# Router work between attention tiles in another order on every engine, and the gates of the first ten tiles on GpSimd

## The reference

```python
x = x + gat(layernorm(x), adj)      # h = n @ W.T + b_W
    # e[i,j] = leaky(h[i]@a1 + h[j]@a2 + b_a), masked by adj, softmax over j, @ h
x = x + moe(layernorm(x))           # logits = n @ Wr + br, the top 2 of 64 experts
    # gates = softmax of the two logits; per expert relu(n @ W1 + b1) @ W2 + b2
    # out = sum over both experts of gate * expert(n)
```

## Time and profile before

| | |
|---|---|
| median of 3 runs | 276.75 us (276.5 to 277.84) |
| profiled execution | 275.88 us, of which the span is 274.1 us |
| granted TensorE clock, mean | 0.925 |
| TensorE busy | 225.7 us (82%) |
| VectorE busy | 207.5 us (76%) |
| ScalarE busy | 179.6 us (66%) |
| GpSimd busy | 166.7 us (61%) |

### The profile page before, as it was taken

One profiled execution on the slowest core, in us unless ns is written; L12 is line 12 of the kernel. 1 busy time (PEld: TensorE's weight loads), 2 busy tenths in 40 slices (PEclk: granted clock), 3 DMA queues, 4 the chain that ended last, 5 costly groups with the idle time before them and its releaser, 6 DMA issues.

```text
span 274.1 us, 6240 instructions
## 1 busy us (share of the span) xinstructions
PE 225.7 (82%) x1863; PEld 214.7 (78%) x1863; DVE 207.5 (76%) x587; ACT 179.6 (66%) x425; POOL 166.7 (61%) x212
## 2 busy tenths in 40 slices
PE   1494899999988999369893569999999999999840
PEld 1354899999978999259782449999999999999740
DVE  6879999999999999913844714889886767666465
ACT  2748989999878978083351516787877777777400
POOL 5870003450879998972878745445888888875600
PEclk9999799999999999957997557999999999999995
DMA  6987664689477570199011122222159710100067
GB/s 160 205 163 148 133 115 79 163 224 236 149 194 196 153 285 22 40 420 383 22 40 43 57 60 63 61 81 58 51 151 312 253 38 33 41 31 29 23 202 268
DMA packets 11120, 36.89 MB, mean 135 GB/s; under 512 B 2256, under 2 KB 2832, under 8 KB 10320
## 3 DMA queue, kind: packets, MB, share of 16 engines
q0 software_dynamic: 5232, 14.98, 23.6%
q1 hardware_dynamic: 5424, 21.11, 22.5%
q10 hardware_dynamic: 432, 0.40, 0.6%
HBM read 39.36 MB, written 5.51 MB: 164 GB/s over the span
## 4 chain that ended last, share of the span: by engine, by line
PE 57%; DVE 21%; issue 6%; DMA 5%; POOL 5%; ACT 2%; SPq 1%; ACTq 1%; POOLq 0%; DVEq 0%
PE bank L1127 16%; PE bank L1139 16%; PE bank L1023 11%; DVE arena L746 6%; PE bank L1007 5%; DVE arena L740 5%; DMA arena<-result 2%; DMA xs<-in_x 2%; POOL table L431 2%; PE bank L972 2%; DVE arena L731 2%; PE bank L1116 1%; PE bank L1042 1%; PE bank L961 1%; DVE rank L790 1%
## 5 line engine op out<-in xcount | busy, mean ns | idle before, releaser
L1023 PE MATMUL bank<-arena 128*128 128x130 f32 x512 | 64.3, 284 | 0.0
L1023 PEld LDWEIGHTS bank<-arena 128*128 128x128 f32 x512 | 62.0, 199 | 0.6 <-ACT arena L577 0.4
L1127 PE MATMUL bank<-arena 128*128 x384 | 60.4, 281 | 0.5 <-ACT arena L642 0.5
L1139 PE MATMUL bank<-w2s,arena 128*128 x384 | 58.8, 276 | 0.2 <-issue 0.2
L1127 PEld LDWEIGHTS bank<-arena 128*128 128x128 f32 x384 | 51.6, 196 | 1.0 <-issue 0.9
L431 POOL DMA_INDIRECT table<-rows_in,pos x32 | 42.4, 1324 | 14.4 <-issue 7.8
L1139 PEld LDWEIGHTS bank<-w2s,arena 128*128 128x128 f32 x384 | 50.6, 192 | 0.6 <-issue 0.6
L899 DVE SCALAR_TENSOR_TENSOR arena<-bank,arena 128x128 f32 x96 | 33.6, 350 | 21.7 <-PE bank L1139 20.2
L647 ACT ACTIVATE arena<-bank,arena 128x128 f32<-128x128 f32 x96 | 35.2, 366 | 18.4 <-PE bank L1127 17.2
L655 ACT ACTIVATE arena<-arena 128x256 f32 x96 | 39.0, 408 | 2.3 <-issue 2.2
L577 ACT ACTIVATE arena<-bank 128x512 f32<-128x512 f32 x64 | 33.8, 596 | 10.2 <-PE bank L1007 10.1
(11 more groups left out here) (195 smaller groups left out, 286.3 us busy)
## 6 DMA issues: line engine op xcount, KB each, us to landing
arena<-in_adj POOLq DMA_DIRECT2D x16, 512.0 KB, 6.6
w2s<-in_w SPq DMA_DIRECT2D x8, 768.0 KB, 4.4
arena<-in_w SPq DMA_DIRECT2D x6, 1024.0 KB, 8.1
arena<-in_w SPq DMA_DIRECT2D x4, 512.0 KB, 5.8
w2s<-in_w SPq DMA_DIRECT2D x4, 512.0 KB, 4.0
xs<-in_x SPq DMA_DIRECT2D x4, 256.0 KB, 6.3
arena<-result SPq DMA_DIRECT2D x2, 512.0 KB, 4.4
arena<-result SPq DMA_DIRECT2D x4, 256.0 KB, 6.0
```

The lines of the kernel that those rows point to most:

```text
L1023: ins = pe.matmul(OB[t % 2][:, 0:D + 2], pt_r[:, t % 2, j, :], h[:, j, :], start=(j == 0), stop=(j == T - 1))
L1127: ins = pe.matmul(hp(p, b), w1u[:, p % UW, P * b:P * b + P], xT_all[:, bass.ds(column, P)], start=True, stop=True)
L1139: ins = pe.matmul(yp(p), hT[:, p % UH, b, :], w2s[:, bass.ds(u, 1), b, :].rearrange("p e d -> p (e d)"), start=(b == 0), stop=(b == HB - 1))
```

## The change

Nothing is computed differently but the first factor of the gates. The edits:

- **VectorE:** top2(q) of groups 0 to 2 moves ahead of leaky in the step (step 8, 12, 14), place(q) behind leaky of the same step, not one step later. Leaky(15) goes ahead of residual(13), and behind it come residual(13), top2(3), residual(14), place(3), top2(4), place(4), residual(15), top2(5) and so on. The gates of groups 0 to 2 leave VectorE.
- **GpSimd:** a new `gates(q)` for groups 0 to 2: 1 + ge, a power of -1, the product and the copy into the rows, after `counts` in steps 8, 12, 14. In each step the scatters now stand first. They move: tile 3 from step 12 to 11, tiles 5 and 6 from 14 to 13, and tile 9 from behind rstd_of(6) to step 15, ahead of it. Rstd_of(7) no longer stands behind tile 9's scatters.
- **ScalarE:** route_b(q) of groups 0 to 2 before evac, not after it. Norm(10) and norm(11) behind evac(13), no longer ahead of it, and so ahead of scores(15). Deviation(13) behind evac(14). After the loop another order of the last groups.
- **TensorE:** route_c(q) of groups 0 to 2 ahead of turn(LAST+4), not behind the attend before it or a step later; route_a(3) behind attend(13), route_b(3) ahead of attend(14), route_a(4), route_b(4) and route_a(5) in attend(15), route_c(5) ahead of group 6. Group 5's logits get a bank of their own (bank 0), as group 6's have.

New tensors and semaphores are left out of the diff.

```diff
@@ -23,9 +23,9 @@
...
     LAST = [START[q + 1] - 1 for q in range(NG)]
-    PLACED = [(0, 0, 9), (0, 1, 10), (0, 2, 11), (0, 3, 12), (1, 4, 13), (1, 5, 14), (1, 6, 14), (1, 7, 15), (2, 8, 15)]
-    NORMED = [(5 + 2 * i, 2 * i) for i in range(5)] + [(14, 10)]
-    LATER = [LAST[q] + 1 if q < 3 else LAST[q] for q in range(NG)]
+    PLACED = [(0, 0, 9), (0, 1, 10), (0, 2, 11), (0, 3, 11), (1, 4, 13), (1, 5, 13), (1, 6, 13), (1, 7, 15), (2, 8, 15), (2, 9, 15)]
+    EARLY = 3
+    NORMED = [(5 + 2 * i, 2 * i) for i in range(5)]
     LNS = [(t, t + 2) for t in range(0, T - 2, 2)] + [(T - 2, T - 1), (T - 1, T)]
@@ -175,14 +175,15 @@
...
         pos = sb("pos", [P, T, TOPK], I32)
-        gd = sb("gd", [P, GRP])
-        ge = sb("ge", [P, GRP])
-        gs = sb("gs", [P, GRP])
+        gd = sb("gd", [P, T])
+        ge = sb("ge", [P, T])
+        gs = sb("gs", [P, T])
+        minus = sb("minus", [P, T])
         gate = sb("gate", [P, TOPK, T])
...
         OB, M0, M1 = bank[4:6], bank[6], bank[7]
-        LB, RB = [M0] * (NG - 1) + [bank[1]], [M1] * (NG - 1) + [bank[2]]
+        LB, RB = [M0] * (NG - 2) + [bank[0], bank[1]], [M1] * (NG - 1) + [bank[2]]
         ends, coded, sides, b1_at = bank[0][0:E, 0:3], bank[4][0:1, 0:2 * WORDS], bank[5], bank[3][:, 0:HB * TAB]
@@ -377,6 +380,7 @@
...
             pool.memset(expo[:, :], -0.5)
+            pool.memset(minus[:, :], -1.0)
             link(pool.memset(ident[:, :], 0.0))
@@ -424,6 +428,16 @@
...

+            def gates(q):
+                rows = slice(START[q], START[q + 1])
+                pool.wait_ge(s_ge, q + 1)
+                link(pool.tensor_scalar(gs[:, rows], ge[:, rows], 1.0, None, ALU.add))
+                pool.tensor_tensor(gate[:, 0, rows], gs[:, rows], minus[:, rows], ALU.pow).then_inc(s_inv, 1)
+                pool.wait_ge(s_inv, q + 1)
+                pool.tensor_tensor(gate[:, 1, rows], ge[:, rows], gate[:, 0, rows], ALU.mult).then_inc(s_weights, 1)
+                pool.wait_ge(s_weights, q + 1)
+                link(pool.tensor_copy(rows_out[:, rows, :, GATE_COL], gate[:, :, rows].rearrange("p k g -> p g k")))
+
             def place(q, t):
@@ -446,18 +460,20 @@
...
             for s in range(T):
+                for q, t, at in PLACED:
+                    if s == at:
+                        place(q, t)
                 if s + 5 < T:
...
                 for q in range(COUNTED):
-                    if s == LATER[q] + 4:
+                    if s == LAST[q] + 5:
                         counts(q)
-                for q, t, at in PLACED:
-                    if s == at:
-                        place(q, t)
+                for q in range(EARLY):
+                    if s == LAST[q] + 5:
+                        gates(q)
             rstd_of(6)
-            place(2, 9)
             rstd_of(7)
@@ -567,10 +583,10 @@
...
                     for q in range(NG):
-                        if b == 2 and t == LATER[q] + 2:
+                        if b == 2 and q < EARLY and t == LAST[q] + 3:
                             route_a(q)
-                    if t >= T - 2 and b == 2:
-                        deviation(t - 1 if t < T - 1 else T - 2)
+                    if t == T - 1 and b == 2:
+                        deviation(T - 2)
                     act.wait_ge(s_pt, 4 * t + b + 1)
@@ -597,9 +613,9 @@
...
             def route_b(q):
-                n = SIZE[q]
+                rows = slice(START[q], START[q + 1])
                 act.wait_ge(s_gd, q + 1)
-                act.activation(ge[:, 0:n], gd[:, 0:n], ACT.Exp).then_inc(s_ge, 1)
+                act.activation(ge[:, rows], gd[:, rows], ACT.Exp).then_inc(s_ge, 1)

@@ -613,20 +629,28 @@
...
                         norm(t + 1)
+                for q in range(EARLY):
+                    if s == LAST[q] + 5:
+                        route_b(q)
+                if s == T - 1:
+                    route_a(3)
                 if s >= 1:
                     evac(s - 1)
-                for q in range(NG):
-                    if s == LATER[q] + 4:
-                        route_b(q)
+                if s == T - 2:
+                    norm(T - 6)
+                    norm(T - 5)
+            deviation(T - 3)
+            route_b(3)
             norm(T - 4)
...
             evac(T - 1)
+            route_a(4)
             norm(T - 2)
...
             deviation(T - 1)
+            route_b(5)
             norm(T - 1)
-            route_b(5)
             route_a(6)
@@ -760,12 +784,12 @@
...
                 link(ins)
-                dve.tensor_tensor(gd[:, 0:n], top8[:, 0:n, 1], top8[:, 0:n, 0], ALU.subtract).then_inc(s_gd, 1)
+                rows = slice(START[q], START[q + 1])
+                dve.tensor_tensor(gd[:, rows], top8[:, 0:n, 1], top8[:, 0:n, 0], ALU.subtract).then_inc(s_gd, 1)
                 for g in range(n):
...
                 dve.wait_ge(s_lg, q + 1)
-                rows = slice(START[q], START[q + 1])
                 link(dve.tensor_copy(idxf[:, rows, :], idx8[:, 0:n, 0:TOPK]))
@@ -778,18 +802,20 @@
...

-                dve.wait_ge(s_ge, q + 1)
-                link(dve.tensor_scalar(gs[:, 0:n], ge[:, 0:n], 1.0, None, ALU.add))
-                link(dve.reciprocal(gate[:, 0, rows], gs[:, 0:n]))
-                dve.tensor_tensor(gate[:, 1, rows], ge[:, 0:n], gate[:, 0, rows], ALU.mult).then_inc(s_gate, 1)
+                if q >= EARLY:
+                    dve.wait_ge(s_ge, q + 1)
+                    link(dve.tensor_scalar(gs[:, rows], ge[:, rows], 1.0, None, ALU.add))
+                    link(dve.reciprocal(gate[:, 0, rows], gs[:, rows]))
+                    dve.tensor_tensor(gate[:, 1, rows], ge[:, rows], gate[:, 0, rows], ALU.mult).then_inc(s_gate, 1)

...
                 link(dve.tensor_reduce(rank[:, :, 0:n], rk[:, :, 0:n, :], AX.X, ALU.add))
-                dve.wait_ge(s_gate, q + 1)
-                dve.tensor_copy(rows_out[:, rows, :, GATE_COL], gate[:, :, rows].rearrange("p k g -> p g k"))
+                if q >= EARLY:
+                    dve.wait_ge(s_gate, q - EARLY + 1)
+                    dve.tensor_copy(rows_out[:, rows, :, GATE_COL], gate[:, :, rows].rearrange("p k g -> p g k"))
                 dve.scalar_tensor_tensor(pos[:, rows, :].rearrange("p g k -> p k g"), idxf[:, rows, :].rearrange("p g k -> p k g"), float(STRIDE),
@@ -822,20 +848,21 @@
...
                     residual(s - 3)
+                for q in range(EARLY):
+                    if s == LAST[q] + 5:
+                        top2(q)
                 leaky(s - 1)
-                if s == T - 1:
-                    residual(T - 3)
-                for q in range(NG):
-                    if s == LATER[q] + 4:
-                        top2(q)
-                    if s == LATER[q] + 5:
+                for q in range(EARLY):
+                    if s == LAST[q] + 5:
                         place(q)
             leaky(T - 1)
+            residual(T - 3)
+            top2(3)
+            residual(T - 2)
             place(3)
-            residual(T - 2)
             top2(4)
+            place(4)
             residual(T - 1)
-            place(4)
             top2(5)
@@ -898,6 +925,7 @@
...

+            dve.wait_ge(s_weights, EARLY)
             dve.wait_ge(s_zero, 2)
@@ -1010,14 +1038,22 @@
...
                     pe.wait_ge(s_x1, t - 1)
-                for q in range(NG):
-                    if t == LATER[q] + 2:
+                for q in range(EARLY):
+                    if t == LAST[q] + 3:
                         route_a(q)
+                if t == T - 2:
+                    route_b(3)
+                if t == T - 1:
+                    route_a(4)
                 for j in range(T):
                     b = j // CB
-                    for q in range(NG):
-                        if j == T // 4 and t == LATER[q] + 2:
+                    for q in range(EARLY):
+                        if j == T // 4 and t == LAST[q] + 3:
                             route_b(q)
+                    if t == T - 1 and j == 8:
+                        route_b(4)
+                    if t == T - 1 and j == 12:
+                        route_a(5)
                     if j % CB == 0:
@@ -1025,7 +1061,7 @@
...
                 pe.wait_ge(s_row, START[q + 1])
-                if q == NG - 1:
+                if q >= NG - 2:
                     pe.wait_ge(s_ea, 4 * T)
@@ -1063,17 +1099,20 @@
...
             for s in range(T):
+                for q in range(EARLY):
+                    if s == LAST[q] + 4:
+                        route_c(q)
                 turn(s)
                 attend(s)
-                for q in range(NG):
-                    if s == LATER[q] + 3:
-                        route_c(q)
-            route_a(5)
+                if s == T - 3:
+                    route_a(3)
+                if s == T - 2:
+                    route_c(3)
             route_c(4)
             route_b(5)
+            route_c(5)
             route_a(6)
             route_b(6)
-            route_c(5)
```

2 lines of the change are left out of this document (added).

## The result

The changed kernel takes 282.5 us (median of four, 282.24 to 286.08) where the kernel before, measured beside it, takes 277.21 us: a ratio of 1.0204, 95% interval 1.015 to 1.0259. The profiled execution is one of 282.24 us with a span of 280.4 us and a mean granted clock of 0.912. Against the profiled execution of before (275.88, span 274.1) that is +6.3 us of span; on the medians it is +5.3. Medians and ratios in this document leave out executions more than 1.5% above the fastest of the same kernel: five of e9's eleven, one of e11's twelve and two of e12's six.

A forecast was written before the change was run, and what follows sets the result against it. VectorE sets the pace up to 117 us, then TensorE stalls behind a norm awaiting GpSimd's rstd. GpSimd's later queue adds 4.5 us to the profiled 275.88, 0.87 under the 276.75 median: 281.3, said as 281; range 272.5 to 285.

The forecast's parts named there:

- Group 0 on VectorE: VectorE's step 8: top2(0) ahead of leaky(7) waits 2.83 us, not 0.48; step 10 starts 1.6 us later.
- Gates on GpSimd, 5.5 us a group: GpSimd's queue: four gate instructions, 1.7 to 1.9 us alone, take 5.5 us beside VectorE's wide operations.
- What waits for it: ScalarE's norm(6) waits for GpSimd until 94.4; VectorE's top2(1) waits 5.1 us, 3.2 of them GpSimd's.
- Norm(10) in its new place: ScalarE: norm(10) waits for rstd_of(5), done at 127.9 behind six scatters; leaky(15) at 131.6, the removed stall back in full.
- rstd_of(6) and norm(12): GpSimd and ScalarE: six scatters ahead, rstd_of(6) starts at 138.6 and norm(12) at 140.1, +4.5 us.
- Sum: All terms on the profiled execution: +4.5 us, with rstd_of(8) starting at 149.4, before at 144.89.
- The experts and SP's loads at nothing: Experts' stage untouched; SP's expert loads, done by 135 and needed after 163, and adjacency loads hidden: no cost.
- The clock: TensorE: sign, clock stays up until the table stage; rival, it falls ahead of route_a(1) or route_a(3), +1 to +3, chance 0.1.
- A rule against the trace: GpSimd scatters beside two-SBUF-input VectorE operations: the skill page's no-contention reading gives +2.9; the trace's holding, kept, gives +4.5.
- The queue holds: Rival, GpSimd: rstd_of(5) done before about 122, stall gone; 270 to 273.3 us, say 271.7; faster has chance 0.2.
- Norm(6) in time: Rival, GpSimd and ScalarE: gates(0) and four scatters held half as often, the 3.2 us vanish; +1.3, 278.0 us, chance 0.13.
- The gates cost nothing: Rival: the moved gate work and the new waits cancel; 276 to 277.5 us, chance 0.09.

The follow-up runs named there:

- e9: The e4 kernel with the change's new places for the scatters: 277.87 us, ratio 1.0032 to the kernel before.
- e11: The e1 kernel with tile 7's two scatters moved from step 15 to step 14: 275.97 us, ratio 0.9946 to the kernel before.
- e12: The e4 kernel run again, unchanged: 272.84 us, ratio 0.9829 to the kernel before.
- e1: The changed kernel with the gates of groups 0 to 2 back on VectorE: 274.86 us, ratio 0.9897 to the kernel before.
- e8: The kernel before with only the gates of groups 0 to 2 moved to GpSimd: 286.85 us, ratio 1.0354.
- e7: The changed kernel with the old order of groups 0 to 2: 281.95 us, ratio 1.015 to the kernel before.
- e6: The changed kernel with filler transposes on TensorE, 26 ahead of route_a(1) and 34 ahead of route_a(3): 283.85 us, ratio 1.023 to the kernel before.
- e2: The changed kernel with the scatters back in their old places, gates still on GpSimd: 284.33 us, ratio 1.0227 to the kernel before.
- e10: A separate test kernel computing nothing of the layer: GpSimd scatters, a power and an addition beside idle VectorE or five kinds of wide operation; a scatter takes 0.95 to 2.95 us.
- e4: The e3 kernel with the old order of groups 0 to 2 as well: 272.88 us, ratio 0.982 to the kernel before.
- e3: The changed kernel with gates back on VectorE and scatters back in their old places: 281.52 us, ratio 1.0112 to the kernel before.
- e5: The e3 kernel with 32 filler transposes on TensorE ahead of route_a(4): 276.38 us, ratio 0.9966 to the kernel before.

## Why the prediction was right

Forecast: 281.0 us and slower; measured: 282.5 and slower. The mechanism was right, a GpSimd queue that reaches its rstd instructions late. On the profiled executions +4.5 was forecast and +6.3 came. Step by step:

- **Group 0 on VectorE.** Top2(0) at 66.94 after a wait of 2.83; measured 67.32 and 3.25. Right. The 0.4 us are the difference that turn(7) has already (62.38 for 62.00), before any of the edits has an effect.
- **Gates on GpSimd, 5.5 us a group.** Measured 5.36 (77.34 to 82.70), and 5.36 for group 1 (109.44 to 114.80). The power on four columns takes 3.06 and not the 1.15 of its nearest row. Right, and e1 and e8 show the gates to be the cost that decides: 7.6 us between the changed kernel and e1. That the figure came out so closely is in part luck: by the same four instructions the queue is held 3.43 and 1.90 us in e7 and e8, where they meet other operations.
- **What waits for it.** nm2(4) done at 94.4, norm(6) waiting about 4, top2(1) at 98.7 after 5.1: measured norm(6) 94.93 after 3.81, top2(1) 99.42 after 5.18. That the 3.2 us were GpSimd's is borne out by e1, where norm(6) is on time and top2(1) waits 1.77 us, close to the 1.9 that were to remain. Group 2's wait was 0.9 and is 0.89.
- **Norm(10) in its new place.** The six scatters of step 13 done at 126.3, rstd_of(5) 127.9, leaky(15) 131.6; measured 127.29, 128.95, 132.66. "The removed stall has come back in full, one tile on" holds, but its cause was told by half. I named the rstd behind scatters. e1 has the same six scatters ahead of rstd_of(5) and no wait at all, because they start at 103.01 and not at 115.09. Of those 12.1 us the gates of group 1 are 5.4; rstd_of(4), done at 105.6 and not at 101.4, is 4.1, of which 1.3 is there since turn(7) and the rest because ScalarE's deviation stood behind the late norm(6) (1.48 us of waiting, until 101.47); and counts(1), held in its instructions, about 2.3.
- **rstd_of(6) and norm(12).** 138.6 and 140.1, measured 139.80 and 141.44. Here the lateness was 1.3 us, and by residual(15) 1.8 (149.96 for 148.2).
- **Sum.** rstd_of(8) forecast at 149.4, measured 151.13: +6.24 for +4.5. No one step has the 1.7 us. The queue is late by 0.4 at the start, 0.5 at norm(6), 0.8 at scores(14), 1.0 at the end of the scatters, 1.3 at norm(12), 1.8 at residual(15): each part of the sum was a little small. The median holds 5.3 of it.
- **The experts and SP's loads at nothing.** 129.27 us for 129.21. Right.
- **The clock.** "Its clock stays up until the table stage" is wrong, twice. Turn(12), after 1.68 us of idle time, ran at 0.53:

```profile
104.76 3.63 PE L1035 MATMUL bank<-ident,arena 128*128 128x128 f32 x16 [1.68 <-DVE arena L770]
```

  It took 1.97 us before. What that costs no run shows, since e6 has it too. Then TensorE waited 4.04 us ahead of route_a(3) and ran turn(14) and attend(14) at a granted clock of 0.59 on the mean (window 130.13 to 140.98). That is the condition of my rival, to which I gave 0.1 and +1 to +3 us. The condition came about, and by the trace the price did not: attend(14) ends at 140.98, norm(12) comes only at 141.44, and against e6 attend(15) starts about 0.1 us later. My reason for a small price, the wait for norm(12), was the right one. What I did not foresee is the clock in attend(15): e6 and e2, which idle ahead of it, lose 1.3 us there, and the changed kernel does not.
- **A rule against the trace.** By what the Trainium skill ("SBUF — State Buffer", Who interferes with whom) infers, I had the six scatters end at 121.8. They ended at 127.29, and e10 shows scatters beside a tensor_tensor with two SBUF inputs at 1.76 to 2.88 us too. The inference that descriptor generation goes on beside such operations doesn't hold here. What the same section says of an operation with at most one SBUF input outside the two-port modes, that it doesn't contend, agrees with e10's 0.95 to 1.10 us beside the one that takes its other input from PSUM. How scatters that end 4.5 us sooner would bring rstd_of(5) only 1.6 us the prediction does not work out.

**The rivals.** *The queue holds* was given 270 to 273.3 us if rstd_of(5) is done by 122. e1 meets its condition (119.86) and norm(6) is in time too, and it lands at 274.86: leaky(15) does follow leaky(14) at once, but norm(12) then waits 4.72 us for its own six scatters, so the gain is given back in part. *Norm(6) in time* never came about while the gates were on GpSimd: norm(6) waits 3.5 to 5.5 us in each such run (changed kernel, e2, e6, e7, e8). *The gates cost nothing* is out by e8.

**What stays open.** That the gates cost the time is shown for the three groups together, not for each. Norms 10 and 11 behind evac(13) weren't tried alone on the kernel before: there evac(13)'s third bank stands behind TensorE's route_a(3), which needs norm(11). Why the order of groups 0 to 2 and the places of the scatters must go together (e1 274.9 and e4 272.9 with both new or both old; e3 281.5 and e9 277.9 with one) is read from the traces. For e3 it is the eight scatters ahead of norm(12) and the clock, and e5 shows the clock's part; for e9 it is the queue's waits for place(0) and place(1), read from one trace and tested by no run. What tells an execution in which the clock falls in attend(14) from one in which it falls in attend(15) the runs don't say.

## What to carry to other kernels

An instruction that is cheap by itself can be the dearest on an engine whose queue is full and which is held by another: here four small GpSimd instructions of 1.9 us held the queue for 5.4 us a group in the changed kernel, and cost the kernel 7 to 8 us. Before work is moved to a queue, look for the short critical instruction that stands behind it, and work out when that one comes, not how busy the engine is on average. Filler on TensorE is worth trying only if TensorE is what ends last after the gap, and then every gap ahead of that place needs it: work that is done sooner may only open the next gap.

## What the hardware showed

- **The scatter and VectorE's inputs (e10).** Beside an idle VectorE 0.96 us; beside 2048-wide scalar_tensor_tensor or tensor_tensor with both inputs in SBUF 1.8 to 2.95; with one input in PSUM 0.95 to 1.10; beside tensor_scalar in bf16 1.01 to 1.28, in float32 1.54 to 2.10. The power on four columns goes from 1.06 to 2.32 in the same way, a small addition from 0.23 to 1.35.
- **The granted clock after a gap.** It was 0.50 after 3.65 us of idle time (e3), and fell after 4.04 us (changed kernel), 4.90 (e2) and 2.39 (e6). It did not fall in e5, whose TensorE did 32 identity transposes (3.66 us) in the same wait. The length of the gap alone doesn't tell: turn(12) took 3.63 us in the changed kernel and 1.97 in e1, after 1.68 us of idle time in both, and in e1 the turn at 108.40 took 3.38 us after 2.23. After the same 2.36 us ahead of route_a(3) the clock was 0.66 in e4 (119.37 to 129.50) and 1.00 in e12 (118.00 to 128.30), two executions of one kernel. What tells these apart the runs don't say.
- **The mean clock is no measure of the time.** Of one kernel, the execution at 0.912 took 272.47 us (e4) and the one at 0.926 took 274.52 (e12): in the second the clock fell where everything waited for TensorE.
